# The last 104 edge blocks in groups of 48, 32 and 24, with another layout of the block ring

## What is computed

```python
# graph attention, on xn = layernorm(x)
h = (xn @ W).reshape(N, H, C)                       # H = 8, C = 256
e = leaky_relu(a_src[src] + a_dst[dst], 0.2)        # a_* = einsum(h, att_*)
m = segment_max(e, dst);  e = exp(e - m[dst])
alpha = e / (segment_sum(e, dst)[dst] + 1e-16)
x = x + segment_sum(h[src] * alpha[:, :, None], dst).mean(axis=1) + bias
# mixture of experts, on t = layernorm(x): top 2 of 8, out = t + sum_e w_e * (gelu(t@w1_e+b1_e)@w2_e+b2_e)
x = x + moe(layernorm(x))
```

## Time and profile before

| | us |
|---|---|
| median of 3 runs | 1065.32 (1064.61 to 1065.62) |
| the profiled execution | 1062.06 |
| its span | 1060.3 |

### The profile page before, as it was taken

One profiled execution on the slowest core, in us unless ns is written; L12 is line 12 of the kernel. 1 busy time (PEld: TensorE's weight loads), 2 busy tenths in 40 slices (PEclk: granted clock), 3 DMA queues, 4 the chain that ended last, 5 costly groups with the idle time before them and its releaser, 6 DMA issues.

```text
span 1060.3 us, 16555 instructions
## 1 busy us (share of the span) xinstructions
PE 706.9 (67%) x3746; PEld 630.5 (59%) x3747; DVE 692.1 (65%) x1935; ACT 355.6 (34%) x831; POOL 672.2 (63%) x705
## 2 busy tenths in 40 slices
PE   4981020436556656765676676699999997779984
PEld 2980010425546545664665576688888886668873
DVE  6898138545675665766777787647769878734552
ACT  3720021427544554332231110123232223345552
POOL 5787777777767777777777730344145256656665
PEclk9555555769886887786898888899999999889998
DMA  9634053668766776665565435198986652556663
GB/s 350 202 73 103 11 128 107 198 183 275 246 216 195 226 235 209 183 199 151 182 185 152 136 92 205 42 390 310 345 303 240 257 180 86 127 90 108 104 105 44
DMA packets 97127, 190.11 MB, mean 179 GB/s; under 512 B 24755, under 2 KB 54910, under 8 KB 95912
## 3 DMA queue, kind: packets, MB, share of 16 engines
q0 software_dynamic: 31680, 70.52, 27.2%
q1 hardware_dynamic: 50364, 72.93, 20.3%
q10 hardware_dynamic: 14960, 45.16, 11.1%
HBM read 124.74 MB, written 64.74 MB: 179 GB/s over the span
## 4 chain that ended last, share of the span: by engine, by line
PE 28%; POOL 26%; issue 17%; DVE 12%; DMA 12%; POOLq 2%; ACT 2%; ACTq 1%; DVEq 0%; SPq 0%
POOL ring L697 22%; PE banks L931 12%; PE banks L1052 9%; DMA out<-ring 6%; POOL starts_table L751 2%; DMA ring<-agg_table 2%; PE banks L885 2%; DMA ring<-node_table,idx 2%; DVE ring L1740 1%; POOL out L809 1%; DVE arena L1695 1%; PE banks L872 1%; PE banks L1127 1%; DMA arena<-in_src 1%; POOLq L802 1%
## 5 line engine op out<-in xcount | busy, mean ns | idle before, releaser
L697 POOL DMA_INDIRECT ring<-node_table,idx x392 | 408.9, 1043 | 123.2 <-issue 115.3
L931 PE MATMUL banks<-arena,ring 128*128 128x160 f32 x1568 | 289.7, 351 | 125.8 <-issue 64.0
L931 PEld LDWEIGHTS banks<-arena,ring 128*128 128x128 f32 x1568 | 270.8, 230 | 145.3 <-issue 145.1
L1213 ACT COPY arena<-banks 128x400 f32<-128x400 f32 x200 | 88.5, 494 | 345.5 <-PE banks L931 212.3
L809 POOL DMA_INDIRECT out<-ring x56 | 89.7, 1602 | 51.1 <-DMA out<-ring 27.8
L1052 PE MATMUL banks<-ring 128*128 128x256 f32 x544 | 120.5, 381 | 0.0
L1052 PEld LDWEIGHTS banks<-ring 128*128 128x128 f32 x544 | 102.5, 190 | 13.4
L1695 DVE TENSOR_TENSOR arena<-hot,arena 128x640 f32<-128x640 f32 x98 | 75.2, 822 | 44.0 <-PE banks L931 43.5
L1111 PEld LDWEIGHTS banks<-ring 128*128 128x128 f32 x448 | 63.0, 205 | 13.0 <-DVE ring L1923 9.6
L1111 PE MATMUL banks<-ring 128*128 128x128 f32 x448 | 64.3, 290 | 7.7 <-DVE ring L1923 7.5
L1127 PE MATMUL banks<-arena,ring 128*128 x224 | 64.8, 415 | 4.6 <-issue 4.6
(11 more groups left out here) (388 smaller groups left out, 1094.0 us busy)
## 6 DMA issues: line engine op xcount, KB each, us to landing
agg_table<-arena ACTq DMA_DIRECT2D x100, 400.0 KB, 3.3
ring<-agg_table SPq DMA_DIRECT2D x25, 1600.0 KB, 8.5
ring<-slot_table SPq DMA_DIRECT2D x56, 130.0 KB, 2.6
ring<-node_table,idx POOLq DMA_INDIRECT x392, 3.3
ring<-in_x SPq DMA_DIRECT2D x8, 640.0 KB, 14.2
arena<-in_L_ffn_w SPq DMA_DIRECT2D x16, 256.0 KB, 8.9
node_table<-ring SPq DMA_DIRECT2D x5, 640.0 KB, 5.5
ring<-in_L_gnn_W ACTq DMA_DIRECT2D x1, 2048.0 KB, 8.9
```

The costliest lines, as they stand in the source:

```text
L697: pool.indirect_dma_start(rows[:, b % ROOM, :], None, node_table, bass.IndirectOffsetOnAxis(idx[:, b:b + 1], 0)).then_inc(got[got_of(g)], 16)
L931: m = pe.matmul(columns[:, k, bass.ds(at * (UNIT * H), SPREAD * H)], lhs[:, k * P:(k + 1) * P], weights, start=False, stop=True, skip_grou ...
L1213: act.copy(stage[j][:, k * SLOTS * H:(k + 1) * SLOTS * H], views[k]).then_inc(drained, 1)
```

## The change

The plan of groups becomes seven of 48, one of 32 and one of 24 blocks, nine groups instead of ten. Block b lies in place (b + SLOT0) % 96 with SLOT0 = 16, so that the last group's 24 blocks lie in places 0 to 23; a group of 48 can now wrap, and its `scores` are then two operations. The rooms of the node stage move accordingly. The last gathers, the steps of the written-out groups and the end of the chain for the last group change as shown. The diff, cut to its core:

```diff
-GROUP_PLAN = ((3, 16),) * 6 + ((2, 16),) * 3 + ((1, 8),)
+GROUP_PLAN = ((3, 16),) * 7 + ((2, 16), (2, 12))
...
+    SLOT0 = -first_of[GROUPS - 1] % ROOM
+    LOOPED = (WHOLE - 1) // 2 * 2 - 2
...
-        at_raw2, at_agg0, at_W = 0, RAW, RAW + AGG
+        at_raw2, at_agg1, at_w1 = 0, RAW, RAW + AGG
+        at_W = LAST_BLOCKS * ROW
         at_raw0 = at_W + 2 * H * C
-        at_x = first_of[GROUPS - 2] % ROOM * ROW
-        at_agg1 = at_x + TILES * D
+        at_x = (first_of[GROUPS - 2] + SLOT0) % ROOM * ROW
+        at_agg0 = at_x + TILES * D
...
+        def slot_of(b):
+            return (b + SLOT0) % ROOM
...
-                    pool.indirect_dma_start(rows[:, b % ROOM, :], None, node_table,
+                    pool.indirect_dma_start(rows[:, slot_of(b), :], None, node_table,
...
-            for g in range(2, GROUPS - 2):
+            for g in range(2, GROUPS - 1):
                 far_blocks(g - 2)
                 gather(g, 0, blocks_of(g))
 
-            gather(GROUPS - 2, 0, blocks_of(GROUPS - 2))
-            far_blocks(GROUPS - 4)
-            gather(GROUPS - 1, 0, blocks_of(GROUPS - 1))
-            for g in range(GROUPS - 3, GROUPS):
-                far_blocks(g)
+            now = first_of[GROUPS - 3] - (first_of[GROUPS - 1] - ROOM)
+            gather(GROUPS - 1, 0, now)
+            far_blocks(GROUPS - 3)
+            gather(GROUPS - 1, now, blocks_of(GROUPS - 1))
+            far_blocks(GROUPS - 2)
+            far_blocks(GROUPS - 1)
...
-            with pe.Fori(0, WHOLE // 2 - 1) as pair:
+            with pe.Fori(0, LOOPED // 2) as pair:
                 for j in range(2):
-                    group(2 * pair + j, pair * (2 * per_group) + j * per_group, j * GB, (j * per_group) % 2, GB, 0, (5, 9, 12, 12))
-            steps_of = {WHOLE - 2: (5, 9, 12, 12), WHOLE - 1: (6, 9, 11, 12), WHOLE: (2, 5, 8, 8), WHOLE + 1: (3, 6, 8, 8),
-                        WHOLE + 2: (3, 5, 7, 8)}
-            for g in range(WHOLE - 2, GROUPS - 1):
-                group(g, first_of[g] // ITER, first_of[g] % ROOM, first_of[g] // ITER % 2, blocks_of(g), g + 1, steps_of[g])
+                    group(2 * pair + j, pair * (2 * per_group) + j * per_group, slot_of(j * GB), (j * per_group) % 2, GB, 0, (5, 9, 12, 12))
+            for g in range(LOOPED, GROUPS - 1):
+                group(g, first_of[g] // ITER, slot_of(first_of[g]), first_of[g] // ITER % 2, blocks_of(g), g + 1,
+                      (5, 9, 12, 12) if g < WHOLE else (4, 8, 8, 8))
             pe.drain().then_inc(whole_done, 1)
             pe.wait_ge(rescaled, GROUPS)
-            blocks(first_of[GROUPS - 1] // ITER, first_of[GROUPS - 1] % ROOM, first_of[GROUPS - 1] // ITER % 2, range(LAST_BLOCKS // QUAD))
+            for b in range(first_of[GROUPS - 1], NB, ITER):
+                blocks(b // ITER, slot_of(b), b // ITER % 2, range(min(ITER, NB - b) // QUAD))
...
+                here = min(nb, ROOM - slot)
+                link(dve.tensor_tensor(edge_z[:, 0:here, :], rows[:, slot:slot + here, D:ROW], score_d[:, b:b + here, :], ALU.add))
+                if here < nb:
+                    link(dve.tensor_tensor(edge_z[:, here:nb, :], rows[:, 0:nb - here, D:ROW], score_d[:, b + here:b + nb, :],
+                                           ALU.add))
...
-                if g < GROUPS - 1:
-                    rescale(g, at, cols)
-                    take_alpha(g)
-                    spreads(g)
-                else:
-                    take_alpha(g)
-                    spreads(g)
-                    rescale(g, at, cols)
+                rescale(g, at, cols)
+                take_alpha(g)
+                spreads(g)
...
             def over_part(t):
                 j = t % RAW_RING
                 dve.wait_ge(raw_in[j], 16 * (t // RAW_RING + 1))
+                if t == 1:
+                    dve.wait_ge(block_done, NB + 1)
```

More of the change, by code:

```diff
@@ L91, in gat_moe_kernel @@
     assert LOOK_UPS[-1][1] == TILES and H * CHUNKS == P and D == 2 * P and C == D and N < TILES * P
-    assert first_of[GROUPS] == NB and WHOLE % 2 == 0 and LAST_BLOCKS % (2 * QUAD) == 0
+    assert first_of[GROUPS] == NB and LOOPED % 2 == 0 and LAST_BLOCKS % (2 * QUAD) == 0 and SLOT0 % ITER == 0
     assert all(kb == GROUP_KB and ch == CHUNKS for kb, ch in GROUP_PLAN[:WHOLE])
     assert all(kb * ch == SHORT for kb, ch in GROUP_PLAN[WHOLE:-1]) and SHORT % ITER == 0 and SHORT == SPREAD_RING * QUAD
-    assert all(first_of[g] % ROOM + first_of[g + 1] - first_of[g] <= ROOM for g in range(GROUPS))
+    assert all((first_of[g] + SLOT0) % ROOM + first_of[g + 1] - first_of[g] <= ROOM for g in range(GROUPS - 2, GROUPS))
     assert SLOTS * H <= 512 and GB % ITER == 0 and TILES % UNROLL == 0 and NS % ACC_RING == 1
@@ L160, in gat_moe_kernel @@
         RAW = HOMES * HOME_COLS
-        at_raw2, at_agg0, at_W = 0, RAW, RAW + AGG
+        at_raw2, at_agg1, at_w1 = 0, RAW, RAW + AGG
+        at_W = LAST_BLOCKS * ROW
         at_raw0 = at_W + 2 * H * C
-        at_x = first_of[GROUPS - 2] % ROOM * ROW
-        at_agg1 = at_x + TILES * D
-        assert LAST_BLOCKS * ROW <= at_agg0 and at_raw0 + 2 * RAW <= at_x and at_agg1 + AGG <= RING
+        at_x = (first_of[GROUPS - 2] + SLOT0) % ROOM * ROW
+        at_agg0 = at_x + TILES * D
+        assert at_w1 + 4 * D <= at_W and at_raw0 + 2 * RAW <= at_x and at_agg0 + AGG <= RING
+        assert at_x <= (first_of[WHOLE - 1] + SLOT0) % ROOM * ROW + GB * ROW
         x_all = ring[:, at_x:at_x + TILES * D].rearrange("p (t d) -> p t d", d=D)
@@ L177, in gat_moe_kernel @@
         o += 2 * D
-        w1_now = [ring[:, o + j * 2 * D:o + (j + 1) * 2 * D].rearrange("p (k n) -> p k n", k=2) for j in range(2)]
-        o += 4 * D
         assert o <= at_x
+        w1_now = [ring[:, at_w1 + j * 2 * D:at_w1 + (j + 1) * 2 * D].rearrange("p (k n) -> p k n", k=2) for j in range(2)]
         o = at_raw2
@@ L187, in gat_moe_kernel @@
         o += 3 * D
-        assert o <= at_agg0
+        assert o <= at_agg1
         SCAN = GL + 5
@@ L711, in far_blocks @@
                                 pool.tensor_copy(far_rows[:, j, :].unsqueeze(1),
-                                                 rows[:, bass.ds(i * ITER % ROOM + 2 * s + j, 1), 0:D])\
+                                                 rows[:, bass.ds(slot_of(i * ITER) + 2 * s + j, 1), 0:D])\
                                     .then_inc(far_rows_ready, 1)
@@ L1012, in group @@
                     for q0, q1 in zip(cuts, cuts[1:]):
-                        blocks(it + i, slot + i * ITER, (parity + i) % 2, range(q0 - i * per_iter, q1 - i * per_iter))
+                        blocks(it + i, (slot + i * ITER) % ROOM, (parity + i) % 2, range(q0 - i * per_iter, q1 - i * per_iter))
                         if q1 == turn:
@@ L1585, in scores @@
                 kb, nb = kb_of(g), blocks_of(g)
-                slot = first_of[g] % ROOM
+                slot, b = slot_of(first_of[g]), first_of[g]
                 dve.wait_ge(got[got_of(g)], got_by(g))
-                link(dve.tensor_tensor(edge_z[:, 0:nb, :], rows[:, slot:slot + nb, D:ROW], score_d[:, first_of[g]:first_of[g + 1], :],
-                                       ALU.add))
+                here = min(nb, ROOM - slot)
[3 more added lines that the diff above has]
+                                           ALU.add))
                 z = edge_z[:, 0:nb, :].rearrange("p (c k) h -> p k c h", k=kb)
```

## The result

The changed kernel takes 1073.58 us (median of 7 runs, 1071.49 to 1075.4), the kernel before 1063.16 in the same job (7 runs, 1058.85 to 1065.62): ratio 1.0091 [1.007, 1.0111], 10.4 us slower. The profiled execution took 1074.17, its span is 1072.5. The forecast was 1075.1, 9.8 more than the 1065.32 that the kernel before had in three earlier runs; 10.4 is measured within one job.

The account below looks back on a forecast made before the run. Gathers on POOL bound the kernel up to group 5, then a VectorE-TensorE ping-pong. A later group 6 and uncovered last 24 blocks outweighed one chain saved: +9.8 us on 1065.32, so 1075.1, range 1068 to 1082.

Parts of the forecast that it names:

- (1): Through group 5: odd groups' wrapped scores are one operation more, 0.43 to 0.56 us, hidden by 7.73 us waiting.
- (2): VectorE's first operation on group 6's gathered rows waits for block 335: at 551.2 instead of 539.11, 12.1 us later.
- (3): From VectorE's first operation on group 6's gathered rows to that on group 7's: 51.7 us, reaching 602.9.
- (4): From VectorE's start on group 7's rows to group 8's: 40.8 us, TensorE deciding, reaching 643.7.
- (5): From VectorE's start on group 8's rows to the edge stage's end: 53.2 us; end at 696.9, 9.8 us later.
- bound of -4: Low end around the summed forecast: 4 us less if TensorE waits less on accumulators in late groups.
- (6): TensorE's clock in the last six quads: sum left unchanged; 3.9 us more if all slow, 0.8 less at full pace.
- rival D: Clock stays low for all last quads and quad 5 of group 7: 5.4 us more, 1080.5; chance 0.10.
- (7): Moved node-stage rooms: tile 3's load comes 2.1 us later, hidden before the second projection; 0 taken.
- rival C: Later load of tile 3 comes through in the node stage: 2.1 us more, 1077.2; chance 0.06.
- Rival A: Faster: edge stage's end hangs on the last gather with one chain behind it, 9.2 us earlier, median 1056.1; chance 0.07.
- rival B: No difference: VectorE's three waits for TensorE in late groups vanish, at most 10.3 us back, 1064.8; chance 0.06.

Follow-up runs that it names:

- with the other steps: Changed kernel with TensorE's service steps altered for groups 5, 6 and 7: 1073.04 us, ratio 1.0094 to the kernel before.
- the run without the wait: Changed kernel without the gathers of blocks 320 to 335, group 6 waiting for 16 fewer: 1063.19 us, ratio 0.9988 to the kernel before.
- the ten-group plan: Changed kernel with five groups of 48 blocks, four of 32, one of 24, and steps to suit: 1063.5 us, ratio 1.0002 in the usual job.

## Why the prediction was right

The size and the sign hold, and so does the mechanism: that the wait of S6 is the loss is shown by experiment, the other steps are read from the trace. By the steps:

- (1) Wrapped scores: 0.29 us more (490.24), hidden; the run with that part alone shows no loss. But the wait ahead of S5 isn't what hides them, as the prediction says: both operations stand behind it, and the turn came 1.84 us after S5, for 1.67 before. The waits for the gathers of the next group take it up (11.51 at S6).
- (2) S6: 63.3 us after S5, where before it was 51.7, so 11.6 later by the plan (forecast 12.1). S6 comes 2.87 us after the start of its last gather, forecast 2.85. That is no constant, though: with the other steps it was 5.35. That S6 is 553.12 and not 551.2 is due to S5, 2.4 later in this execution. It isn't the new places: in kernels with the old ones S5 lay between 487.4 and 489.7 too.
- (3) S6 to S7: 52.0, forecast 51.7.
- (4) S7 to S8: 40.8, as forecast; the factors 27.0 after S7 (26.7), 4.2 to the first spread, the rest 9.6 (9.8).
- (5) S8 to E: 50.8, forecast 53.2. This is where the sum was off. Scores and pieces were served 1.6 us sooner, the join took 7.9 instead of 8.2, six quads took 18.6 instead of 19.5, and only the last `rescale` waited longer, 1.11 instead of 0.7. The steady pace was right: 3.03 us from one quad to the next (691.41 to 694.44), copied as 3.05. What I took too long are the first quads after an idle: three took 8.59 at 637.99, and I had copied 9.36. The windows of these three quads, before and after, have the granted clock in the third column from the end:

```profile
608.50:617.90 9.40, 9.35 (x48) 9.12 (x48) 8.38 (x18) 1.71 (x4) 7.29 (x7) 0.72 0.55 167
...
638.00:646.60 8.60, 8.58 (x48) 8.34 (x48) 8.12 (x19) 0.00 (x0) 0.00 (x0) 0.78 1.01 398
```

  So the time of these quads went with the granted clock (9.82 us at a mean of 0.68, 9.66 at 0.70, 9.36 at 0.72, 8.59 at 0.78), and not with waits on accumulators, of which the prediction's bound of -4 speaks: TensorE was busy nearly all of both windows. Step (6) put six quads "all at the full pace" at 18.7 without a row; they took 18.6 with the first 3.6 us at 0.50, so 18.7 is no bound of that kind.
- (6) Clock: in the idle before the last group it was 0.59, then 0.50, its lower level, for the first 3.6 us; from 690 to 696.7 it was 1.00, and four quads took 13.2 us to the next one's start, against the 14.0 I took. Quad 5 of group 7 took 2.44 (647.13). So rival D is out. The Trainium skill, "TensorE: Matmul & The Clock Gate", section "Why this matters for your kernels", warns of idle between bursts of matmuls. The trace agrees: 0.50 after the idle.
- (7) Rooms: `over_part(1)` waited until 696.99 and was done at 700.4, before its projection; tile 3's load was issued 3.8 us after E, 2.5 later than before relative to E (forecast 2.1).

```profile
696.99 1.05 DVE L1740 COPY ring<-ring 128x448 f32<-128x448 f32 x2 [13.10 <-PE banks L939]
...
700.53 0.37 SPq L567 DMA_DIRECT2D ring<-agg_table  x1
```

  No projection waited for them: counted from E, the starts of the projections are the same in both kernels for 73.6 us (13.8, 20.7, 34.5 and so on). The first difference is 0.7 us, at 82.4 (before 81.7), and with the same rooms but other steps it was 81.7 again. So rival C is out.

The offsets cancel: the cycle of S5 to S6 brought 11.6 later, S6 to E 4.4 earlier (143.6 for 148.0; forecast 2.3), which makes 7.2, and the late S5 of this execution 2.4, together 9.6 at E. So the agreement of 9.6 with 9.8 is partly luck of one execution. The medians differ by 10.4, which includes the node stage, and I can't say which of the parts carries the rest.

Rival A is out, since S8 came at 645.91 and waited for no gather; rival B too, since VectorE's waits for TensorE stayed (3.57, 4.20, 2.97).

Why large groups lose here: a group's chain starts when its last block has come, and the 48 blocks of a group take POOL 63 us to gather, while the two other engines need 52 for them (1.08 us a block). They overtake, and then stand idle, TensorE with quads 6 to 12 of the group before still to do. A group of 32 needs 42 us of gathers and 39 to 41 of work. The kernel before goes over to 32 where the engines are level with the gathers; the change goes over one group later and buys with it one chain fewer: 11.6 us for 4.4, both counted to E (the medians of the run without the wait don't show the 4.4, see above).

## What to carry to other kernels

A larger batch saves fixed work but starts only when its last input is there: compare, batch by batch, the time its inputs take to come with the time its work takes, and where the inputs take longer, the batch size sets an idle, whatever it saves. Removed work counts only in the cycle in which it sets the pace: 11.5 us less on VectorE were worth at most 4.4. And a service moved forward helps only as far as the next wait behind it; look for that wait first. And look at the transfer that all wait for: with quads and a store beside it the last gather landed 2.5 us later than alone, though it isn't shown that they were the reason.

## What was not expected

In four jobs all kernels took far longer: the one before 159 to 173 us (1222.55 to 1235.73), the changed one 143, the ten-group plan 211. One of these jobs ran on a chip that had given 1064.57 for the kernel before in an earlier job. There the changed kernel, expected at 1.007 to 1.011 again, was faster than the one before, 1216.39 against 1234.43, ratio 0.9855 [0.9823, 0.9887]; the ten-group plan was slower (1.0335 [1.0303, 1.0366] and 1.0332 [1.0298, 1.0365]). The waits of the changed kernel in such a job, by engine, line and what ended them: us in total, times, longest.

```profile
DVE arena L1575 <- remote: 57.3, 1, 57.3
...
DVE piece_m L1635 <- remote: 42.6, 5, 11.4
DVE arena L1707 <- remote: 34.8, 4, 10.7
```

"Remote" is what no engine, queue or semaphore of this core explains; in the usual execution no engine has such a wait. The wait of 57.3 at L1575 is one of 1.0 there. The busy time of VectorE is the same (680.2 us, usual 680.6): it isn't slower, it stands still, in single pauses, and TensorE pauses within a quad. The number of instructions doesn't explain who loses how much: the kernel before (16555) and the ten-group plan (16553) have as good as the same, and lose 171 and 211 us in one and the same job. What ends these pauses isn't in the profile, and I have no experiment that shows it. Comparisons from those jobs decide nothing above.
